# What the gathers wait for: memsets and products, or the gather two ahead in line

## The reference

```python
e = jnp.stack([tbl_0[ids[:, 0]], tbl_1[ids[:, 1]], ..., tbl_38[ids[:, 38]]], axis=1)
p, q = e[:, ROW, :], e[:, COL, :]                    # 741 pairs
z = jnp.einsum('bpc,apc,bpa->bp', p, w, q)
h = jnp.concatenate([z, dense_ctx], axis=1)
h = jnp.maximum(h @ W_top1 + b_top1, 0.0)            # 757 -> 512
h = jnp.maximum(h @ W_top2 + b_top2, 0.0)            # 512 -> 256
y = h @ W_top3                                       # 256 -> 1
```

## Time and profile before

| what | value |
|---|---|
| median of 3 runs | 795.97 us (794.8 to 798.86) |
| the profiled execution | 796.05 us, of it the span 794.2 us |
| TensorE matmul busy | 732.0 us, 92% |
| VectorE busy | 637.3 us, 80% |
| ScalarE busy | 104.3 us, 13% |
| GpSimd busy | 422.5 us, 53%: 384 gathers 379.3, 75 memsets 43.3 |
| DMA | 142.02 MB, mean 179 GB/s |
| packets of the gathers' queue | 12288, 32 per gather |

### The profile page before, as it was taken

One profiled execution on the slowest core, in us unless ns is written; L12 is line 12 of the kernel. 1 busy time (PEld: TensorE's weight loads), 2 busy tenths in 40 slices (PEclk: granted clock), 3 DMA queues, 4 the chain that ended last, 5 costly groups with the idle time before them and its releaser, 6 DMA issues.

```text
span 794.2 us, 11392 instructions
## 1 busy us (share of the span) xinstructions
PE 732.0 (92%) x4418; PEld 291.8 (37%) x4418; DVE 637.3 (80%) x797; ACT 104.3 (13%) x186; POOL 422.5 (53%) x463
## 2 busy tenths in 40 slices
PE   1688686999979999999999999999999999999998
PEld 0232222333333344444333444444333443443343
DVE  4658698999978999878978898879969887778650
ACT  3232111011100010101111010110111010011002
POOL 6899999943556555545556555455656455100000
PEclk9879798999999999999999999999999999999999
DMA  7544429587888636356765555347765455443300
GB/s 213 167 149 157 125 88 299 207 293 260 282 293 289 224 99 232 97 187 191 251 214 163 193 166 190 117 154 234 232 219 168 144 158 181 163 144 92 116 1 0
DMA packets 71553, 142.02 MB, mean 179 GB/s; under 512 B 13301, under 2 KB 22600, under 8 KB 71372
## 3 DMA queue, kind: packets, MB, share of 16 engines
q1 hardware_dynamic: 49228, 118.04, 43.4%
q10 hardware_dynamic: 9984, 16.94, 6.0%
q0 software_dynamic: 12288, 6.32, 5.3%
HBM read 110.25 MB, written 31.00 MB: 178 GB/s over the span
## 4 chain that ended last, share of the span: by engine, by line
PE 74%; DVE 11%; issue 6%; DMA 4%; POOL 3%; ACT 2%; SPq 1%; ACTq 0%; DVEq 0%
PE z_ps L610 24%; PE u_ps L586 23%; PE t_ps L549 10%; PE m_ps L623 8%; DVE prod L910 6%; DVE one_hot L898 4%; POOL e_rows L409 3%; PE m_ps L625 3%; PE t_ps L530 2%; DMA scratch<-parts 1%; DMA e<-scratch 1%; PE u_ps L645 1%; PE u_ps L654 1%; PE m_ps L627 1%; PE m_ps L637 1%
## 5 line engine op out<-in xcount | busy, mean ns | idle before, releaser
L910 DVE TENSOR_TENSOR prod<-u_ps,eT 128x1024 f32<-128x1024 f32 x400 | 469.9, 1216 | 96.0 <-PE u_ps L586 95.4
L409 POOL DMA_INDIRECT e_rows<-in_tbl_dram,idx x384 | 379.3, 988 | 257.5 <-DVE prod L910 184.9
L586 PE MATMUL u_ps<-e,w 128*128 128x512 f32 x800 | 256.5, 434 | 21.9 <-DVE prod L910 11.6
L610 PE MATMUL z_ps<-prod,sel 128*32 128x512 f32 x1600 | 262.8, 612 | 0.0
L586 PEld LDWEIGHTS u_ps<-e,w 128*128 128x128 f32 x800 | 133.2, 190 | 160.8 <-DVE prod L910 76.7
L549 PE MATMUL t_ps<-one_hot,tb 125*32 125x512 bf16 x1560 | 155.0, 398 | 14.4 <-DVE one_hot L898 14.2
L898 DVE TENSOR_SCALAR one_hot<-hot_idx,row 125x512 bf16<-125x512 f16 (+2 forms) x320 | 137.1, 482 | 11.4 <-PE t_ps L549 9.5
L549 PEld LDWEIGHTS t_ps<-one_hot,tb 125*32 125x32 bf16 x1560 | 55.9, 99 | 112.1 <-issue 68.0
L610 PEld LDWEIGHTS z_ps<-prod,sel 128*32 128x32 f32 x1600 | 43.8, 109 | 139.7 <-issue 108.8
L623 PE MATMUL m_ps<-zT,w1s 128*128 128x512 f32 x144 | 73.5, 592 | 0.0
L714 ACT CAST parts<-t_ps 128x512 fp32r<-128x512 f32 (+1 forms) x40 | 23.4, 586 | 238.1 <-PE t_ps L549 144.1
(11 more groups left out here) (53 smaller groups left out, 133.1 us busy)
## 6 DMA issues: line engine op xcount, KB each, us to landing
w<-w_rows SPq DMA_DIRECT2D x100, 512.0 KB, 5.9
e<-scratch SPq DMA_DIRECT2D x62, 512.0 KB, 4.8
scratch<-parts SPq DMA_DIRECT2D x62, 256.0 KB
w_rows<-h ACTq DMA_DIRECT2D x48, 256.0 KB
e_rows<-in_tbl_dram,idx POOLq DMA_INDIRECT x384
hot_idx<-hot SPq DMA_DIRECT2D x12, 512.0 KB
h<-in_w_dram ACTq DMA_DIRECT2D x12, 256.0 KB, 3.7
e<-scratch SPq DMA_DIRECT2D x8, 384.0 KB, 4.2
```

Of the source, the lines that this page charges most:

```text
L409: pool.indirect_dma_start(e_rows[:, r, n, D * q:D * q + D], None, tables[f], bass.IndirectOffsetOnAxis(ap=idx[:, t, f * TPG + n:f * TPG + ...
L586: last = nc.tensor.matmul(u_ps[:, s % 2, place, :], w4[:, p % WR, (u % PW) * P:(u % PW + 1) * P], e4[:, E4_SLOT[g], j - C * g, :], start=T ...
L610: last = nc.tensor.matmul(z_ps[D * quad:D * quad + D, z % 2, :], sel[:, D - 1 - row:2 * D - 1 - row], prod[:, (NS * t + n) % PR, place, :] ...
L910: nc.vector.tensor_tensor(prod[:, s % PR, :, :], u_ps[:, s % 2, :, :], e, ALU.mult).then_inc(s_mul, 1)
```

## The change

Every gather from the 21st on waits until the gather two ahead of it in line has landed. For this each slot has two semaphores, one for gathers of even and one for those of odd number, so that a count is not mixed with that of the neighbour in flight. `landed(n)` is the count that gather n's semaphore shows when it has landed. The memsets, `s_pause` and the wait for products are gone. The turn waits for both semaphores of its slot. The wait for a free slot stays.

```diff
-PACED_FROM, PACE_LEAD = 96, 40
...
-PAUSES = PACED_FROM - 1 - sum(TPG * len(gathered(c)) for c in GATHERED[:2])
-
-
-def rows_count(c):
-
-    n = GPOS[c]
-    return sum(16 * TPG * len(gathered(GATHERED[x])) for x in range(n % ER, n + 1, ER))
+WINDOW = 2
+GATHERS = [c for c in GATHERED for k in range(TPG * len(gathered(c)))]
+
+
+def landed(n):
+
+    return 16 * len([m for m in range(n % WINDOW, n + 1, WINDOW) if (GPOS[GATHERS[m]] - GPOS[GATHERS[n]]) % ER == 0])
+
+
+def last_gathers(c):
+
+    return [max(n for n in range(w, len(GATHERS), WINDOW) if GATHERS[n] == c) for w in range(WINDOW)]
...
-        s_rows = [sem(f"s_rows{r}") for r in range(ER)]
+        s_rows = [[sem(f"s_rows{r}_{w}") for w in range(WINDOW)] for r in range(ER)]
...
-                        if issued >= PACED_FROM:
-                            pool.wait_ge(s_mul, issued - PACE_LEAD + 1)
+                        if GPOS[c] > 1:
+                            before = issued - WINDOW
+                            pool.wait_ge(s_rows[GPOS[GATHERS[before]] % ER][before % WINDOW], landed(before))
                         pool.indirect_dma_start(
                             e_rows[:, r, n, D * q:D * q + D], None, tables[f],
                             bass.IndirectOffsetOnAxis(ap=idx[:, t, f * TPG + n:f * TPG + n + 1], axis=0),
-                        ).then_inc(s_rows[r], 16)
+                        ).then_inc(s_rows[r][issued % WINDOW], 16)
                         issued += 1
-                        if GPOS[c] > 1 and issued < PACED_FROM:
-                            if paused:
-                                pool.wait_ge(s_pause, paused)
-                            nc.gpsimd.memset(pause[:, :], 0.0).then_inc(s_pause, 1)
-                            paused += 1
...
-                        sp.wait_ge(s_pause, PAUSES)
...
-                pe.wait_ge(s_rows[GPOS[c] % ER], rows_count(c))
+                for n in last_gathers(c):
+                    pe.wait_ge(s_rows[GPOS[c] % ER][n % WINDOW], landed(n))
```

More of the change, by code:

```diff
@@ L308, in tower @@
         y_sb = h1[0:1, 0, :]
-        pause = w1s[:, 0, :]
         zroom = zT[:, 1, :, :].rearrange("p k n -> p (k n)")
@@ L382, in tower @@
         s_y = sem("s_y")
-        s_pause = sem("s_pause")
         def e_slot(t, g):
@@ L396, in _ @@
             pool.wait_ge(s_idx, 16)
-            paused = 0
             issued = 0
```

## The result

| | before | changed |
|---|---|---|
| median | 797.08 us (794.8 to 798.86, 4 runs) | 833.72 us (831.33 to 837.68, 4 runs) |
| ratio | | 1.0466, 95% interval 1.0428 to 1.0505 |
| profiled execution, its span | 796.05, 794.2 us | 831.33, 829.4 us |
| mean granted clock | 0.974 | 0.951 |

The change costs 36.6 us. The forecast was 802.5 us with a range to 820, so it had the sign and missed the size. A second measurement, beside three other kernels, gave 835.27 us and 1.0449 (1.0414 to 1.0483). In the first group of later runs, e1 to e4, the kernel before took 815 us in place of 797, so three of its kernels were measured again as e9, e10 and e12, and where the two disagree the second counts; why it was slow is not known.

A forecast was written before the change was run, and what follows sets the result against it. TensorE was taken to bound later tiles, with VectorE, copies and DMAs sharing the first tile's bound. The sum -5.7 + (5.7 + 2.2) + 4.2 = +6.4 us on 796.05 gave 802.5 us, range 788 to 820.

The forecast's parts named there:

- Item 1: First tile: without memsets 79 VectorE compares lose 171 ns each, 13.5 us in all, of which 5.7 us shorten the run.
- The chain's share of the compares: Compares are 17.0% of the chain of waits from 34 to 155 us, 20.6 us; 171/613 of it gives 5.7 us.
- The bounds, 0 and 13.5: Limits of the memsets' gain in us: none if copies and DMAs fill the room, 13.5 if all of it counted.
- Item 2: Gather stream: two in flight set the pace, 1.82 us per gather before 167 us, 2.25 in the loaded stretch, 1.84 later.
- The correction from 1.93 to 1.84: Later tiles: measured averages give 1.93 us per gather, lowered to 1.84 because waiting gathers are seldom issued into a blocked moment.
- the loaded stretch: First tile's part with DMA engines 84% busy, 187 to 252 us; pace there taken as 2.25 us, up to 2.35.
- the fixed 2.0 us: Skill's rule for a GpSimd-issued DMA: 2.04 us per 16 KB gather, so the window never binds and the sum is 790.
- Item 3: Turn of (1,3), end of the loaded stretch: TensorE waits 8 us for gather 131's rows, turn at 254.7, 2.2 us later.
- Item 4: Later tiles: 96 gathers at 1.84 us take 176.6 us against 174.5, +2.1 us per tile, twice, +4.2 us.
- Much slower: Rival, chance 0.15: measured averages hold uncorrected, 2.35 us per gather in the loaded stretch and 1.93 later; +27.5, or 823.5 us.
- The signs that the prediction named for being right: Gathers paced by landings at 1.8 to 2.3 us, compares about 440 ns, some 8 us wait at (1,3), smaller at (2,3), (3,3).

The follow-up runs named there:

- e1: The changed kernel with each gather waiting for the one three ahead in place of two; 967.51 us in the disturbed first group.
- e4: The changed kernel with no wait for landings, only for a free slot; 1098.73 us, ratio 1.3482, in the disturbed first group.
- e9: The changed kernel with a window of three in place of two, measured again in a later group; 790.69 us, ratio 0.9897.
- e10: The changed kernel with the window of two only up to gather 95, then the old product waits, measured again; 787.95 us, ratio 0.9868.
- e12: The changed kernel with only the wait for a free slot, measured again in a later group; 791.34 us in a single execution.
- e5: The changed kernel again, with no edit; 835.27 us, ratio 1.0449.
- e7: The kernel before, memsets and product waits kept, with the window of two from gather 132 on; 825.51 us, ratio 1.0331.
- e6: The kernel before, memsets kept, with the window of two for gathers 96 to 131 only, product waits after; 804.36 us, ratio 1.0071.
- e11: The changed kernel with weights of tiles 2 to 4 loaded into one partition of 128, so results are wrong; 808.42 us, ratio 1.0112.

## Why the prediction was right in sign and wrong in size

**Item 1, the memsets: right in mechanism, under-sized.** The compares fell from 613 to 437 ns, as forecast (442). Of the 13.9 us that this frees (79 x 176 ns), 9.8 were gained by the turn of (0,9), not 5.7, and 8.8 in e10. The chain's share of the compares was too low a measure of what of them lies on the path. The bounds, 0 and 13.5, held. No other kind of VectorE's work changed: a product takes 1210 ns before and 1214 after in this stretch, an operation on two SBUF tensors (L864) 678 and 680. The Trainium skill, SBUF — State Buffer, "SBUF: two separate sides", describes a port pair that one of GpSimd and VectorE locks for a whole instruction, against VectorE's instructions in a two-port mode, and against those with two SBUF inputs only where GpSimd's reads SBUF. The trace agrees in that only the 16-bit compares gained beside memsets, which have no input.

**Item 2, the pace: the step that failed.** The forecast's 1.84 us for the later tiles is (3.41 + 0.27) / 2: a gather in flight for 3.41 us, and 0.27 us from a landing to the next issue. Measured are 1.945 and 1.938. The step that failed is the second term. The prediction took it from one quiet moment, the landing of the indices; it is the quickest case, and not the mean. The semaphores of the changed kernel's trace give 3.43 us in flight for gathers 132 to 323, as forecast, and 0.47 us on the mean from a landing to the issue that waits for it, with a median of 0.26. 0.20 us more, over a window of two, is 0.10 us per gather and 19 us over two tiles. e5 gives 3.44 and 0.50, e7 3.48 and 0.48.

Where the 0.20 us come from: of these 192 gathers 62 begin over 0.3 us after the landing that they wait for. 48 of them stand right behind their neighbour: the landing came while GpSimd was still at the neighbour, and in this trace no two gathers begin less than 1.24 us apart. The other 14 are the first of their chunk, which has the slot's wait too. Of the 40 us that all 62 lose, 28 are the neighbours' and 12 the chunks'. The chain of waits from 302 to 307 us shows both kinds of issue:

```profile
301.06 4.17 DMA e_rows<-in_tbl_dram,idx
305.24 0.26 issue
305.50 0.94 POOL e_rows L408
306.44 0.30 issue
306.74 3.96 DMA e_rows<-in_tbl_dram,idx
```

The gather of 305.50 us begins 0.26 us after a landing. That of 306.74 waits for the gather of 302.92, which landed at 305.41; it begins 1.33 us after that, because it stands behind its neighbour.

The correction from 1.93 to 1.84 was not what failed. That "a gather that waits for landings is seldom issued into a blocked moment" is borne out in size: the packets of gathers 132 to 323 end on the mean 2.76 us after the issue in the kernel before, 2.57 in the changed one and 2.61 in e5. That is 0.15 to 0.19 us less, 0.08 to 0.10 per gather; the correction took 0.09. What it leaves open is how a window of two goes through a blocked moment that comes all the same. GpSimd's timeline of the changed kernel:

```profile
309.03 0.94 POOL L408 DMA_INDIRECT e_rows<-in_tbl_dram,idx  x1 [1.35 <-DMA e_rows<-in_tbl_dram,idx]
310.96 1.00 POOL L408 DMA_INDIRECT e_rows<-in_tbl_dram,idx  x1 [0.99 <-DMA e_rows<-in_tbl_dram,idx]
316.04 0.94 POOL L408 DMA_INDIRECT e_rows<-in_tbl_dram,idx  x1 [4.08 <-DMA e_rows<-in_tbl_dram,idx]
```

Between 310.96 and 316.04 us nothing is issued. Of the 192 intervals from gather 131 to 323, 27 are over 3 us and take 110.8 us; before 12 did, with 38.8 us. The kernel before goes on issuing through such a moment (7 issued, 3 moved) and so keeps its pace.

For the loaded stretch the forecast had 2.25 us, (4.23 + 0.27) / 2. In e6, whose gathers 96 to 131 begin nearly where the forecast put them, it is 2.54, with 4.56 us in flight and 0.58 to the next issue: there both terms were too small. For the stretch before 167 us it took 1.82, which no row gave; from gather 20 to 96 it was 1.99 (3.5 us in flight), since the stretch isn't light: from 117 to 184 us 28 gathers took 67 us, 2.4 us each. Gather 96 began at 183.66 us, not 171.7.

What makes the landings late enough to matter is the other traffic: e11 takes away weights alone, the time in flight falls from 3.43 to 3.00 us, and the loss of the later tiles is gone. The Trainium skill, DMA: Bandwidth & Descriptors, "Latency and other measured facts", has the HBM's part of a DMA's fixed cost grow with the load. The trace agrees in that a gather is in flight for less time beside less traffic, and 3.43 us is far from the fixed 2.0 us by which the window would never bind; whether the HBM or the DMA engines make it longer, no run separates.

**Item 3, the turn of (1,3): place right, 7.8 us short.** The wait is there, 11.46 us in place of 8, and the turn stands at 262.50 in place of 254.7. Gather 96 is 12.0 us later than worked out; from 96 to 131 the pace was 2.185, not 2.25 (-2.3 us), and the turn came 2.4 us after the last issue, not 4.2 (-1.8). That is the sum, not the cause: e6 began gather 96 at 169.63 us and gained only 1.6 us at the turn. With its 2.54 us the forecast's own start gives gather 131 at 260.6, and it was issued at 260.14. The term that was too small is the loaded pace. What the text didn't see is that (1,0) waits too, for 6.14 us. It lies inside the same delay and adds nothing to it.

**Item 4, the other tiles: form right, size wrong.** A late tile takes 96 times the pace, as it said: 96 x 1.945 and 96 x 1.938 are 186.7 and 186.0 us, and the turns of (1,3), (2,3) and (3,3) are 186.8 and 185.9 apart. At 1.84 it had 176.6. That is 10.2 and 9.3 us too little, 19.5 of the miss of 28.8.

**The clock, not in the sum.** After the wait for (1,3) TensorE runs slower for a while:

```profile
252.00:262.50 10.50, 0.00 (x1) 0.03 (x1) 0.00 (x0) 0.00 (x0) 6.49 (x8) 0.59 0.13 30
262.50:280.00 17.50, 17.50 (x94) 7.68 (x97) 14.03 (x20) 1.66 (x3) 8.95 (x10) 0.85 0.57 191
```

TensorE stands still from 251.04 to 262.50 us. The granted clock falls to the lower level, 1.2 GHz, at 253.97 us and is back at 2.4 GHz at 267.63, which gives the 0.59 and the 0.85 of the two stretches; the four matmuls of each late turn take 1.01 to 1.09 us in place of 0.66. From the turn of (1,3) to that of (1,4) this costs 1.9 us. It costs the total little, because the next turns are set by the stream and not by TensorE; only what is lost behind (3,3) counts, 1.6 us: the next turn stands 43.56 us behind it, before 41.93.

The miss: 7.8 + 10.2 + 9.3 + 1.6 = 28.9 us, against 829.4 - 800.6 = 28.8 of span.

**The rivals.** "Much slower", with 0.15, was the case that came: it took the averages without the correction and gave 823.5 us, 7.8 under the profiled execution: 4.1 at (1,3), 2.1 in the two tiles and 1.6 behind (3,3). Its pace of 1.93 was within 1% of the measured one, but by luck: it has 3.6 us in flight and 0.27 to the next issue, the runs 3.43 and 0.47, and the two errors cancel. The signs that the prediction named for being right (a pace of 1.8 to 2.3 us, compares of 440 ns, a wait at (1,3) and smaller ones later) all came, since they could not tell 1.84 from 1.94; against a limit of 1.818 that was the whole question.

## What to carry to other kernels

A window of landings makes the pace (mean time in flight + mean time from a landing to the next issue) / window. Put means into both terms, not the quiet moment: a landing that comes while the engine is still issuing the neighbour is used late, and with the slots' waits that made 0.47 us out of 0.27. And give it a window that leaves room: here two lost 4.6%, three gained 1.0%. A pace that is tied to the consumer goes on issuing through blocked moments, a window stands still in them. And work that only passes time on one engine (75 memsets) can slow another's: without them the first tile gained 9 us, and that kept to the end in e10.

## What was not expected of the hardware

- A gather of 16 KB took 3.0 us on the mean from issue to its last packet beside a DMA share of 0.54, and 2.5 to 2.6 beside 0.34 to 0.36; its median in the changed kernel was 2.4 and 2.2 us in the two tiles, so the tail makes the mean.
- In the group of e1 to e4, gathers issued back to back went with a nearly idle TensorE (6.86 us busy of 29), and VectorE stood idle for up to 35.2 us before a product. In e12 the same kernel shows nothing of it (55.56 of 56 us). Why that group hit the kernels with long bursts so much harder (967 and 1099 us) than the kernel before (815) stays open.
- Once the stream is late, the delay is carried to the end in full: e6 is 9.2 us late at the last turn as at the first behind its window.
